# Weights prepared in another order and on other engines, a table moved up its queue, and the last four output tiles handled another way

## The reference

```
xn = layernorm(x)                                  # layer 0
x  = x + attention0(xn) + ffn0(xn)                 # causal softmax attention, with layernorm(out + v) @ Wfc; relu MLP, 256-1024-256
xn = layernorm(x)                                  # layer 1
x  = x + gated_attention(xn) + experts(xn)         # groups of 64 with rope, ending in layernorm(out @ Wo + bo) * ln2_w + ln2_b
                                                   # 8 experts with LoRA, the best 2 of each token, silu(h1) * h3
```

## Time and profile before

| what | us |
|---|---|
| three runs | 1121.52, 1117.2, 1113.53 |
| median | 1117.2 |
| the profiled execution | 1116.3 |
| its span, first to last instruction | 1114.6 |
| outside the span | 1.7 |

### The profile page before, as it was taken

The page is one execution under the profiler, slowest core; times in us unless marked ns, Lnnn a source line. Parts: engine busy times, 40 slices in busy tenths (PEclk is TensorE's granted clock), DMA queues, the critical chain, the costliest instruction groups (busy, mean ns, idle before and its releaser), DMA issues.

```text
span 1114.6 us, 20433 instructions
## 1 busy us (share of the span) xinstructions
PE 1055.8 (95%) x6338; PEld 915.2 (82%) x6338; DVE 781.8 (70%) x1741; ACT 393.5 (35%) x770; POOL 434.6 (39%) x416
## 2 busy tenths in 40 slices
PE   5999999999999996995899899999999999999995
PEld 4899999999999996864677788888888888877874
DVE  5688787878788676754565777777777777764745
ACT  2636463555446363431211222222222222442300
POOL 2846454555447331045575100000011010088886
PEclk8999999999999998897899999999999999999998
DMA  9364672666468346425466446534355252265456
GB/s 272 97 206 130 187 244 101 192 160 202 140 190 205 123 148 185 126 76 171 151 189 214 166 136 223 171 116 142 101 194 166 78 194 58 84 123 86 68 95 141
DMA packets 113780, 168.61 MB, mean 151 GB/s; under 512 B 17296, under 2 KB 87568, under 8 KB 113552
## 3 DMA queue, kind: packets, MB, share of 16 engines
q1 hardware_dynamic: 93328, 120.09, 35.5%
q0 software_dynamic: 20352, 47.23, 15.3%
HBM read 96.14 MB, written 71.14 MB: 150 GB/s over the span
## 4 chain that ended last, share of the span: by engine, by line
PE 87%; DVE 4%; issue 2%; another core or an unknown queue 2%; DMA 2%; SPq 1%; POOL 1%; ACT 0%; DVEq 0%; POOLq 0%; ACTq 0%
PE wide L549 19%; PE wide L1900 17%; PE bank L549 11%; PE bank L1900 9%; PE wide L1398 7%; PE bank L1398 3%; PE bank L1925 3%; PE wide L1458 3%; PE wide L1482 2%; PE bank L1482 2%; PE bank L640 1%; PE bank L1893 1%; PE wide L1471 1%; PE wide L1468 1%
## 5 line engine op out<-in xcount | busy, mean ns | idle before, releaser
L1900 PE MATMUL wide<-expert_ring,xsT 128*128 x642 | 170.5, 401 | 3.1 <-DVE xsT L1989 2.3
L1900 PEld LDWEIGHTS wide<-expert_ring,xsT 128*128 128x128 f32 x642 | 113.3, 188 | 23.4 <-issue 3.9
L1958 ACT ACTIVATE gsT<-bank 128x512 fp32r<-128x512 f32 x71 | 42.5, 599 | 242.3 <-PE bank L1925 242.3
L1783 POOL DMA_DIRECT2D expert_ring<-experts_scratch x24 | 17.3, 720 | 264.7 <-issue 137.6
L2001 DVE TENSOR_TENSOR slots_h<-wide,expert_bias 128x512 f32<-128x512 f32 x71 | 49.1, 691 | 68.0 <-PE wide L1900 67.8
L1347 POOL DMA_INDIRECT slot_rows_scratch<-ring,slot x64 | 69.2, 1081 | 52.0 <-DVE slot L1734 32.0
L532 POOL TENSOR_TENSOR folded_matrix<-fold,folded_matrix 128x512 fp32r<-128x512 f32 x48 | 64.0, 1341 | 42.5 <-ACT folded_matrix L726 39.7
L549 PE MATMUL wide<-xnT,w 128*128 128x512 f32 x234 | 60.3, 399 | 0.0
L1900 PEld LDWEIGHTS bank<-expert_ring,gsT 128*128 128x128 f32 x432 | 56.1, 189 | 3.5 <-issue 0.3
L944 DVE TENSOR_TENSOR hT<-hid,hT 128x512 fp32r<-128x512 f32 x64 | 54.6, 860 | 5.9 <-ACT hid L781 5.1
L549 PE MATMUL wide<-xnT,pT 128*128 128x512 f32 (+2 forms) x288 | 58.6, 348 | 0.0
(11 more groups left out here) (284 smaller groups left out, 2589.1 us busy)
## 6 DMA issues: line engine op xcount, KB each, us to landing
experts_scratch<-folded_matrix SPq DMA_DIRECT2D x24, 1024.0 KB, 5.5
expert_ring<-experts_scratch POOLq DMA_DIRECT2D x24, 1024.0 KB, 6.0
raw<-in_expert_weights SPq DMA_DIRECT2D x24, 512.0 KB, 7.5
xs_ring<-slot_rows_scratch SPq DMA_DIRECT2D x71, 128.5 KB, 2.1
slot_results_scratch<-ys_ring SPq DMA_DIRECT2D x71, 128.0 KB, 2.2
slot_rows_scratch<-zeros SPq DMA_DIRECT2D x23, 385.5 KB, 7.5
ring<-xn_scratch SPq DMA_DIRECT2D x32, 257.0 KB
xn_scratch<-u SPq DMA_DIRECT2D x16, 512.0 KB, 7.8
```

Source lines behind the costliest of these rows:

```text
L1900: ins = mm(o, parts[i], moving, start=(first and q == 0), stop=(last and q == 2))
L1958: return nc.scalar.activation(o, i, ACT.Copy)
```

## The change

1. **Weights.** `prepare_weights` becomes three functions. `weights_alone` runs before NM:0's wait for the reciprocal root: beta's rows, and the low part of Wv, whose high part ACT now copies ahead of all else. `attention_weights` runs behind NM:0. `centred_weights` (subtract the row means from Wfc, split Wfc) runs behind DVE's PT:2. PE makes its small products in `wide0` instead of three other buffers, makes the one of row means behind XT:1, and waits for each part where it is first used (VV, PT, S, FC) instead of all together ahead of XT:0.
2. **W1 before W2.** W2 gets its own semaphore. ACT copies W1 as soon as it has landed, ahead of its first XT, and W2 behind XT:3 instead of XT:1. POOL subtracts W1 behind its first power, ahead of its first bias addition and of both sets of factors; W2 stays behind FA:1.
3. **Tables.** The loads of `turn` and Wo are parted: LC:1 (`turn`) follows LC:0, behind LW:5; LC:3 (Wo) stands where both were, behind SM:5.
4. **Last four tiles** (12 to 15 of the second half). PE puts the bias row into the bank with a product of a row of ones and `bo`, ahead of the four products. DVE takes bn_stats and the first operand of YF straight from the bank; the addition goes, and a wait for an earlier tile moves from YS to YF. SX:3 becomes four stores of one tile, each with its own wait.

```diff
+FROM_BANK = 12
@@ SP, start
-        sp.dma_start(w20[:], ...).then_inc(ffn_w_in, 16)
+        sp.dma_start(w20[:], ...).then_inc(ffn_w2_in, 16)
@@ POOL, VA
                 tt(rs[:], ve[:], half[:], ALU.pow).then_inc(rstd_ready, 1)
                 if b == 0:
-                    pool.wait_ge(attn_split, 1)
+                    pool.wait_ge(ffn_high, 1)
+                    tt(w1[:, 1, :, :], w10, w1[:, 0, :, :], ALU.subtract).then_inc(ffn_split, 1)
+                    pool.wait_ge(attn_split, 2)
@@ POOL, FA:1
-                    pool.wait_ge(ffn_high, 1)
-                    tt(w1[:, 1, :, :], w10, w1[:, 0, :, :], ALU.subtract).then_inc(ffn_split, 1)
                     pool.wait_ge(ffn_high, 2)
                     tt(w2[:, 1, :, :], w20[:], w2[:, 0, :, :], ALU.subtract).then_inc(ffn_split, 1)
@@ PE, start
-        pe.wait_ge(scaled_fc, 1)
-        for c in range(DC):
-            last = mm(G[2][:, 0:DIM], average, wfc0[:, c, :], start=(c == 0), stop=(c == DC - 1))
-        last.then_inc(pre_done, 1)
-        pe.wait_ge(wqk_split, 1)
-        pe.wait_ge(attn_split, 2)
+        def row_means():
+            pe.wait_ge(scaled_fc, 1)
+            pe.wait_ge(attn_split, 2)
+            for c in range(DC):
+                last = mm(S[:, 512:512 + DIM], average, wfc0[:, c, :], start=(c == 0), stop=(c == DC - 1))
+            last.then_inc(pre_done, 1)
@@ PE, XT
+                if b == 0 and n == 1:
+                    row_means()
@@ PE, PT:0 / VV:0 / S:0 / FC:0 of batch 0
+                    pe.wait_ge(wqk_split, 1)
-                    pe.wait_ge(attn_split, 4)
+                    pe.wait_ge(attn_split, 1)
+                    pe.wait_ge(attn_split, 3)
+                    pe.wait_ge(attn_split, 4)
@@ ACT, start
+        act.wait_ge(const_in, 80)
+        copy(wv[:, 0, :, :], wv0).then_inc(wv_high, 1)
         act.wait_ge(pre_done, 1)
-        nc.scalar.activation(wqk..., G[0], ACT.Copy, scale=1.0 / 16.0
+        nc.scalar.activation(wqk..., S[:, 0:512], ACT.Copy, scale=1.0 / 16.0
                              ).then_inc(wqk_high, 1)
-        act.wait_ge(const_in, 80)
+        act.wait_ge(ffn_w_in, 16)
+        copy(w1[:, 0, :, :], w10).then_inc(ffn_high, 1)
@@ ACT, XT
-                if b == 0 and n == 1:
-                    act.wait_ge(ffn_w_in, 32)
-                    copy(w1[:, 0, :, :], w10).then_inc(ffn_high, 1)
+                if b == 0 and n == 3:
+                    act.wait_ge(ffn_w2_in, 16)
                     copy(w2[:, 0, :, :], w20[:]).then_inc(ffn_high, 1)
@@ DVE, NM and PT
+                if b == 0 and n == 0:
+                    weights_alone()
                 dve.wait_ge(rstd_ready, b + 1)
                 for t in range(4 * n, 4 * n + 4):
                     ts(xn[:, t, :], ...)
                 if b == 0 and n == 0:
-                    prepare_weights()
+                    attention_weights()
...
                 low(lambda i: pT[...], g_bank(u), u, taken=taken_g)
+                if b == 0 and n == 2:
+                    centred_weights()
@@ orders on SP
-        LC:0 LC:1 LX:0 LC:2 RG:0 ...
+        LC:0 LC:1 LC:3 LX:0 LC:2 RG:0 ...
-    "sync": "LW:5:1 SM:5:1",
+    "sync": "LW:5:2 SM:5:1",
@@ SP, LC
                 sp.dma_start(turn[:], io["turn"]).then_inc(row_in, 16)
+            elif kind == "LC" and n == 3:
                 sp.wait_ge(*dense["rows_weighed"])
                 sp.dma_start(wo1[:], ...).then_inc(keep["late_in"], 16)
@@ SP, SX
+                if half and n == 2 * NB - 1:
+                    for t in range(*rows_of.indices(TPB)):
+                        sp.wait_ge(x_ready, T0 + TPB * b + t + 1)
+                        sp.dma_start(to[:, t, :], x[b][:, t, :]).then_inc(stored[n], 16)
@@ PE, YY
+                biased = half and n >= FROM_BANK
+                if biased:
+                    mm(o[:, 0:DIM], keep["ones"][0:1, :], keep["bo"][0:1, :], start=True, stop=False)
@@ DVE, YS and YF
+                if half and n >= FROM_BANK:
+                    own(nc.vector.bn_stats(sty[:, i, :], g_full(dve, ("YY", n))[:, 0:DIM]))
+                else:
...
+                if half and n >= FROM_BANK:
+                    hold(dve, v_held, x_ready, T0 + n - 3)
+                    rows_from = G[g_use(("YY", n))[0]][:, 0:DIM]
-                own(stt(out=y[:, i, :], in0=y[:, i, :], scalar=mvy[:, i, 0:1], in1=row("ln2_w"), ...))
+                own(stt(out=y[:, i, :], in0=rows_from, scalar=mvy[:, i, 0:1], in1=row("ln2_w"), ...))
```

More of the change, by code:

```diff
@@ L555, in tensor @@
             for kc in range(DC):
-                last = mm(G[0][:, c * DIM:(c + 1) * DIM], wqT[:, kc, c * P:(c + 1) * P], wkT[:, kc, :],
+                last = mm(S[:, c * DIM:(c + 1) * DIM], wqT[:, kc, c * P:(c + 1) * P], wkT[:, kc, :],
                           start=(kc == 0), stop=(kc == DC - 1))
@@ L817, in prepare_weights, with attention_weights @@
             last.then_inc(beta_spread, 1)
-            own(tt(crow[:], rows[:, 0, :], rows[:, 1, :], ALU.add))
+            dve.wait_ge(wv_high, 1)
+            tt(wv[:, 1, :, :], wv0, wv[:, 0, :, :], ALU.subtract).then_inc(attn_split, 1)
+            nc.vector.memset(average, 1.0 / DIM)
+        def attention_weights():
             dve.wait_ge(wqk_high, 1)
             flat = [wqk[:, i, :, :].rearrange("p c d -> p (c d)") for i in range(2)]
-            stt(out=flat[1], in0=G[0], scalar=1.0 / 16.0, in1=flat[0], op0=ALU.mult, op1=ALU.subtract
+            stt(out=flat[1], in0=S[:, 0:512], scalar=1.0 / 16.0, in1=flat[0], op0=ALU.mult, op1=ALU.subtract
                 ).then_inc(wqk_split, 1)
+            own(tt(crow[:], rows[:, 0, :], rows[:, 1, :], ALU.add))
             dve.wait_ge(pre_done, 2)
-            tt(crow[:], crow[:], G[1][:, 0:DIM], ALU.add).then_inc(attn_split, 1)
-            nc.vector.memset(average, 1.0 / DIM)
             for c in range(DC):
@@ L828, in prepare_weights, with centred_weights @@
             last.then_inc(scaled_fc, 1)
-            own(nc.vector.tensor_copy(wv[:, 0, :, :], wv0))
-            tt(wv[:, 1, :, :], wv0, wv[:, 0, :, :], ALU.subtract).then_inc(attn_split, 1)
+            tt(crow[:], crow[:], S[:, 512:512 + DIM], ALU.add).then_inc(attn_split, 1)
+        def centred_weights():
             dve.wait_ge(scaled_fc, 1)
@@ L833, in prepare_weights @@
             for c in range(DC):
-                last = tt(wfc0[:, c, :], wfc0[:, c, :], G[2][:, 0:DIM], ALU.subtract)
+                last = tt(wfc0[:, c, :], wfc0[:, c, :], S[:, 512:512 + DIM], ALU.subtract)
             last.then_inc(attn_split, 1)
-            dve.wait_ge(attn_split, 3)
+            hold(dve, v_held, attn_split, 3)
             own(nc.vector.tensor_copy(wfc[:, 0, :, :], wfc0))
@@ L1310, in unit @@
             elif kind == "EN":
-                for q4 in range(2 * NB):
+                for q4 in range(2 * NB - 1):
                     sp.wait_ge(stored[q4], 16 * (half + 1))
+                sp.wait_ge(stored[2 * NB - 1], 16 * (1 + TPB // 2))
                 sp.wait_ge(z_stored, 16 * 2 * NB)
@@ L1480, in unit @@
                 o, done = g_bank(un)
+                biased = half and n >= FROM_BANK
+                if biased:
+                    mm(o[:, 0:DIM], keep["ones"][0:1, :], keep["bo"][0:1, :], start=True, stop=False)
                 for e in range(EC):
-                    last = mm(o[:, 0:DIM], oT[:, h % 2, e, n % 4 * P:(n % 4 + 1) * P], wo1[:, e, :], start=(e == 0),
-                              stop=(e == EC - 1))
+                    last = mm(o[:, 0:DIM], oT[:, h % 2, e, n % 4 * P:(n % 4 + 1) * P], wo1[:, e, :],
+                              start=(e == 0 and not biased), stop=(e == EC - 1))
                 last.then_inc(done, 1)
@@ L1670, in unit @@
                 i = n % 2
-                if n >= 4:
-                    hold(dve, v_held, x_ready, T0 + n - 3)
-                tt(y[:, n % 4, :], g_full(dve, ("YY", n))[:, 0:DIM], row("bo"), ALU.add).then_inc(g_free(("YY", n))[0], 1)
-                hold(dve, v_held, *g_free(("YY", n)))
-                own(nc.vector.bn_stats(sty[:, i, :], y[:, n % 4, :]))
+                if half and n >= FROM_BANK:
+                    own(nc.vector.bn_stats(sty[:, i, :], g_full(dve, ("YY", n))[:, 0:DIM]))
+                else:
+                    if n >= 4:
+                        hold(dve, v_held, x_ready, T0 + n - 3)
+                    tt(y[:, n % 4, :], g_full(dve, ("YY", n))[:, 0:DIM], row("bo"), ALU.add).then_inc(g_free(("YY", n))[0], 1)
+                    hold(dve, v_held, *g_free(("YY", n)))
+                    own(nc.vector.bn_stats(sty[:, i, :], y[:, n % 4, :]))
                 own(nc.vector.bn_aggr(mvy[:, n % 4, :], sty[:, i, :]))
@@ L1682, in unit @@
                 dve.wait_ge(rstd_ready, T0 + n + 1)
-                own(stt(out=y[:, i, :], in0=y[:, i, :], scalar=mvy[:, i, 0:1], in1=row("ln2_w"), op0=ALU.subtract,
+                rows_from = y[:, i, :]
+                if half and n >= FROM_BANK:
+                    hold(dve, v_held, x_ready, T0 + n - 3)
```

(2 more changed lines are left out.)

16 lines of the change are left out of this document (8 added, 8 removed).

## The result

The changed kernel takes 1110.9 us, the median of 20 runs (1108.1 to 1113.8), against 1116.9 us for the kernel before beside it: a ratio of 0.9945, 95% interval 0.9935 to 0.9955, or 6.1 us less. The profiled execution took 1110.5 us with a span of 1108.8 us; the span of before was 1114.6.

What follows compares the result with a forecast made beforehand. PE, busy 1055.8 of 1114.6 us, was taken as the bound; 0.9 + 5.0 + 0.3 = 6.2 us took the profiled 1116.3 to 1110.1, and the median's 0.9 above that execution gave 1111.0, range 1103 to 1118.

Steps and rivals of the forecast that it cites:

- The table: Between the layers: earlier `turn` removes DVE's 4.97 us wait, so PE's norm comes sooner; 5.0 us, bounds 2.5 and 9.
- x1's store: Between the layers: N1:2 needs it landed, expected near 437.4, just in time; as late as before, the gain is 2.5 us.
- the clock: Between the layers: a shorter PE wait could keep the clock up, at most 4 us more; no gain was taken.
- The start: PE's path to W1:0: reordered weights bring W1:0 from 37.19 to near 36.3; 0.9 us, bounds a loss of 1 and 2.5.
- EP:0 starts at about 27.1: At the start: EP:0, which needs POOL's factors, was to start at about 27.1 against 27.99 before.
- 1.6 of the 2.5 us: At the start, before EP:0: 1.6 of PE's 2.5 us go into a new wait on POOL, 0.9 stay.
- The last tiles: At the end: POOL's gathers and powers keep the last tile hardly sooner; 0.3 us, bounds -0.3 and 1.5.
- DVE's YS:15 done 1.5 us earlier relative to PE: At the end: sign that DVE finishes this step 1.5 us earlier, then idles until POOL's last powers.
- Swallowed later: First attention: rival that PE's waits there grow by the gain between the layers, giving 1116; chance 0.15.
- Slower: First attention: rival that shifted instruction fetches add another stall on DVE or ACT, giving 1122; chance 0.08.
- More than forecast: Rival: clock stays up between layers (4 us more) or an attention stall is avoided (5 to 6), 1102 to 1107; chance 0.2.

Runs made afterwards that it cites:

- table: Kernel before with part 3 alone (`turn` loaded behind LC:0, Wo behind SM:5): ratio to before 0.9954, 5.2 us.
- w1late: Kernel after with POOL's subtraction for W1 moved behind the first factors: ratio to before 0.9962.
- weights: Kernel after with the table and the last tiles as before, so only parts 1 and 2 are left: ratio to before 0.9991.
- stores: Kernel after with z's last four tiles also stored singly, in turn with x's: ratio to before 0.9948.
- early: Kernel after with LoRA matrices loaded ahead of W1, first expert weights ahead of W2, POOL's first factors ahead of W1's subtraction: 1092.0 us, ratio to before 0.9935.
- tail: Kernel before with part 4 alone (bias on PE, read from the bank, single stores): ratio to before 1.0006.
- after_again: Kernel after run once more, unchanged, on another chip: 1096.5 us, ratio to before 0.9959.

## Why the prediction was right

1111.0 us were predicted, 1110.9 measured. The large term was right in its cause and its size. That the sum is met to 0.1 us is luck: the two small terms, 1.2 us together, are nowhere to be seen in the traces, and about 1 us that no term named came in their place between 550 and 626 us.

- **The table, 5.0 us: right.** `turn` was issued at 409.77 (forecast: near 410), the norm started at 437.98 (438.0), PE waited 3.3 us (3.1). "table" alone gave 5.2 us, and 4.86 at the norm. x1's store did not become the wait; the clock gave nothing for certain: it was at 0.50 from 440 to 445 and at 0.53 from 445 to 450, and the first of the queries' products behind the norm came the same 4.9 us sooner (447.55 against 452.49). From 450 to 455 it was at 1.00 instead of 0.50, and the next such product came 5.4 us sooner (450.82 against 456.23), but 0.4 of this was gone again at the stall of 547.25.
- **The start, 0.9 us: right up to EP:0, wrong behind it.** "EP:0 starts at about 27.1" was 26.22, and a new wait on POOL there was foreseen as "1.6 of the 2.5 us". It was 3.7, because PE was through PT:2 at 22.5 instead of the forecast 25.5: VV:0 started at 18.09, not near 20, and took 1.65 us at the granted clock 1.00 instead of the 2.90 that it had taken at 0.50. Faster PE work ahead of a fixed arrival made only a longer wait. I blamed POOL's order; "w1late" showed the load of the LoRA matrices. Then the trace lost what EP:0 had gained, in two steps. Behind the wait the granted clock fell to 0.50, so that XT:2, XT:3 and VV:1 took 1.91 + 2.42 us instead of the 1.04 + 1.62 of the kernel before. And PT:1, forecast 0.3 us earlier than before, started at 32.80 instead of 32.16, 0.64 later: `centred_weights` on DVE ahead of XT:2's low part took 3.0 us (28.38 to 31.42), not 2.0, with POOL's factors now beside it, and DVE's first fold ahead of it had waited for the expert weights to 27.18, although EP:0 was done at 26.8. The wait of before for W1 (0.62 us) is gone, and this makes W1:0 even. In "weights", "w1late" and "stores" PE waits 1.76, 1.47 and 1.36 us at this place. POOL's subtraction beside DVE's norms (5.40 us for 1.4) was charged with nothing either; it cost PE nothing, because PE stood waiting for POOL. The trace gives 0.0 us at W1:0, the runs of "weights" 1.0 with 1.8 to either side, so that the term is neither confirmed nor refuted. That a gain at the start is kept until the next layer shows better in "early": 3.0 us at W1:0, and its norm between the layers starts PE at 435.98 instead of 438.96.
- **The last tiles, 0.3 us: not seen.** The runs hold 0.3 as well as nothing, and the traces show nothing: "tail" gave a loss of 0.7 us with 1.7 to either side, and no tail of the five kernels that have part 4 as it stands is shorter than that of before. The mechanism was right: POOL's powers and gathers set the end. Its power for tile 10 still waits for DVE (0.50 us, to 1088.96; before, to 1094.93); from there on POOL waits for nobody, and the span ends 19.84 us later (before, 19.67), whatever PE and DVE saved. As forecast, DVE's second-last tile waits for POOL's power (0.47 us) and the four stores stand behind SZ:3. The sign "DVE's YS:15 done 1.5 us earlier relative to PE" was a poor one, since PE itself ends later: it is 4.2 us relative to PE, and 0.7 relative to the last gather. The bias product costs more than the 0.47 us a tile that was taken: the products of two tiles start 2.55 us apart where before it was 1.73, so 0.82 each. It is indeed hidden. The runs without one half or the other give 0.1 us for the bank, up to DVE's last result, and nothing for the stores.

The bias product, in PE's timeline of the kernel after, and the reading from the bank in DVE's:

```profile
1091.41 0.69 PE L1511 MATMUL bank<-bo,ones 1*128 1x256 f32 x2
1092.04 1.99 PE L1513 MATMUL bank<-wo,oT 128*128 128x256 f32 x8
...
1094.07 0.43 DVE L1703 BATCH_NORM_STATS2 sty<-bank 128x6 f32<-128x256 f32 x1 [1.25 <-PE bank L1513]
...
1098.63 0.48 DVE L1721 SCALAR_TENSOR_TENSOR y<-bank,mvy,ln_w 128x256 f32<-128x256 f32 x1
```

Statistics and product took 0.43 and 0.48 us from the bank, as they had from SBUF; the fixed extra cost of a PSUM source that the Trainium skill gives ("VectorE: DVE Perf Modes", the TRN2 errata) is in none of these rows, and the sum was right to leave it out.

Of the rivals, *Swallowed later* is refuted: the output product of tile 10, behind all the attention, starts at 1085.32 instead of 1091.28, 5.96 us sooner, which is the whole gain, the unforeseen 1 us included. *Slower* did not come: the stall of the earlier trace rows was 21.5 us on ACT instead of 17.3, but PE lost only 1.9 us more, and the kernel after has this stall on one chip and not on another, so the change does not make it. *More than forecast* did not come either.

## What to carry to other kernels

When a step is moved forward, follow it to the next thing that arrives at its own time, a load above all, and price the gain by that; here two loads of 288 and 512 KB issued ahead of those of 1024 KB, with POOL's step for the first, brought W1:0 forward by 3.0 us in the trace, the rewrite of the weights' preparation by 0.0. When work is put behind a step on one engine, look at what stands behind it there: `centred_weights` delayed the low parts that PE needed next. A forecast that is met to the decimal is no proof of its small terms; follow the lead from place to place. Before work is given to POOL early, look at which DVE instructions with all operands in SBUF it will lie beside. Here splitting the stores shortened the tail only when their places in the queue followed the order in which the data came ready (8.67 us against 9.52).

## What the hardware showed that was not expected

- POOL's 4.6 us subtraction in SBUF stretched four small DVE instructions from 1.24 or 1.38 us to 5.40 (4.87 in "early"), but not one that reads a bank. Beside POOL's factors, the cast and subtraction of Wfc took 1.04 and 1.04 us; with POOL idle ("early") 0.43 and 0.69.
- The same program was faster on other chips, the kernel after by 14 us and the kernel before by 16 to 21; for the kernel after, stalls in one place account for it.
- The granted clock at the start differs between executions of nearly the same program: VV:0 took 1.62 us in one profile, 2.90 before and 3.08 in "stores". Executions can so differ by 3 to 4 us at W1:0 (37.4 and 41.3 in "after_again" and "stores", whose starts are the same). In "table" VV:0 took 2.90 us although the clock is recorded as 1.00 there, so the record does not always show at which level PE ran.
- A product with one row and 256 columns was no cheaper on PE than one with 128 rows: its two records took 0.63 us to the start of the next (1091.41 to 1092.04), eight records of the other kind 1.92 (to 1093.96), or 0.48 for two.
